# Output bias added to the residual rows by GpSimd instead of by a matmul; two places for the parts of attended rows; one-pass spread of the inverse denominators

## The reference

```python
q = (x @ wq_w.T + wq_b).reshape(b, t, H, HD)      # H = 32 heads of HD = 32
k = (x @ wk_w.T + wk_b); v = (x @ wv_w.T + wv_b)  # one key and value head
scores = jnp.einsum('bqhd,bkd->bhqk', q, k1) / jnp.sqrt(jnp.float32(HD))
scores = jnp.where(causal, scores, -jnp.inf)
attn = jnp.einsum('bhqk,bkd->bqhd', softmax(scores), v1).reshape(b, t, H * HD)
x = _layernorm(x + attn @ wo_w.T + wo_b)          # x: 2 x 2048 x 1024, float32
x_sim = clip(x * x_scale, -448, 448)              # x_scale = 448 / max|x|, w alike
out = _layernorm(x + x_sim @ w_sim * (1 / (x_scale * w_scale)))
```

## Time and profile before

| | |
|---|---|
| runs of the kernel | 2508.66, 2510.32, 2511.88 us; median 2510.32 |
| the profiled execution | 2512.94 us, of which the span of its instructions is 2511.2 |
| PE | busy 2408.2 us, 96% |
| DVE | busy 1750.0 us, 70% |
| ACT | busy 1299.4 us, 52% |
| POOL | busy 802.8 us, 32% |

### The profile page before, as it was taken

One profiled execution on the slowest core, in us unless ns is written; L12 is line 12 of the kernel. 1 busy time (PEld: TensorE's weight loads), 2 busy tenths in 40 slices (PEclk: granted clock), 3 DMA queues, 4 the chain that ended last, 5 costly groups with the idle time before them and its releaser, 6 DMA issues.

```text
span 2511.2 us, 36167 instructions
## 1 busy us (share of the span) xinstructions
PE 2408.2 (96%) x14312; PEld 1559.2 (62%) x14312; DVE 1750.0 (70%) x1294; ACT 1299.4 (52%) x1412; POOL 802.8 (32%) x441
## 2 busy tenths in 40 slices
PE   6999999699999999999999999999999995999998
PEld 5888887245555555555555555555555554888887
DVE  6334335798887888888888888888788884444444
ACT  2222223576777777777776776777777662000000
POOL 2232221022232322232223232322233232556653
PEclk9999999899999999999999999999999997999999
DMA  7433433342232122212222222122212211222221
GB/s 235 142 117 138 154 126 122 94 119 60 74 64 50 43 64 55 54 43 64 51 56 43 52 57 64 43 52 56 65 43 64 51 68 67 84 89 91 88 87 64
DMA packets 150742, 198.01 MB, mean 79 GB/s; under 512 B 8558, under 2 KB 108878, under 8 KB 148558
## 3 DMA queue, kind: packets, MB, share of 16 engines
q1 hardware_dynamic: 126990, 144.71, 22.2%
q10 hardware_dynamic: 23616, 51.39, 5.3%
HBM read 123.72 MB, written 72.35 MB: 78 GB/s over the span
## 4 chain that ended last, share of the span: by engine, by line
PE 66%; DVE 7%; ACT 5%; issue 3%; POOL 1%; ACTq 0%; DVEq 0%; POOLq 0%
PE bank L1233 18%; PE bank L1245 16%; PE bank L1308 14%; PE bank L1218 12%; DVE acc L1000 6%; ACT prob L761 4%; PE bank L1255 2%; PE bank L1263 2%; PE bank L1298 1%; PE bank L1215 1%; ACT att_hi L748 0%; DVE res L974 0%; DVE stats L816 0%; DVE r_den L961 0%; POOL prob L609 0%
## 5 line engine op out<-in xcount | busy, mean ns | idle before, releaser
L761 ACT ACTIVATE prob<-bank 128x1024 f32<-128x1024 f32 x1088 | 1054.9, 1022 | 442.2 <-PE bank L1233 435.3
L1000 DVE TENSOR_TENSOR acc<-acc,prob 128x2048 f32<-128x2048 f32 x420 | 988.3, 2353 | 107.0 <-ACT prob L761 88.7
L1233 PE MATMUL bank<-q_st,keys 98*128 98x512 f32 x2176 | 644.8, 415 | 33.6 <-ACT prob L761 22.1
L1233 PEld LDWEIGHTS bank<-q_st,keys 98*128 98x128 f32 x2176 | 377.0, 189 | 367.9 <-ACT prob L761 264.0
L1245 PE MATMUL bank<-prob,v_t 128*32 128x512 f32 x4352 | 526.3, 602 | 0.0
L609 POOL TENSOR_SCALAR_AFFINE_SELECT prob<-prob 128x1024 f32<-128x1024 f32 x128 | 184.1, 1461 | 736.2 <-ACT prob L761 736.2
L1245 PEld LDWEIGHTS bank<-prob,v_t 128*32 128x32 f32 x4352 | 114.0, 109 | 263.6 <-issue 253.0
L996 DVE TENSOR_TENSOR acc<-prob 128x2048 f32<-128x2048 f32 x60 | 137.6, 2293 | 153.9 <-ACT prob L761 139.5
L1132 PE MATMUL bank<-xt_hi,w_hi 128*128 128x512 f32 x576 | 227.6, 395 | 14.8 <-DVE xt_lo L837 14.1
L1132 PE MATMUL bank<-xt_hi,w_lo 128*128 128x512 f32 x576 | 227.1, 394 | 0.0
L1132 PE MATMUL bank<-xt_lo,w_hi 128*128 128x512 f32 x576 | 226.7, 394 | 0.0
(11 more groups left out here) (112 smaller groups left out, 2555.9 us busy)
## 6 DMA issues: line engine op xcount, KB each, us to landing
q_st<-q_hi_d SPq DMA_DIRECT2D x128, 256.0 KB
xt_raw<-x_t SPq DMA_DIRECT2D x16, 1024.0 KB, 6.9
q_hi_d<-part_hi ACTq DMA_DIRECT2D x64, 256.0 KB, 2.1
q_lo_d<-part_lo ACTq DMA_DIRECT2D x64, 256.0 KB, 2.3
q_st<-q_lo_d SPq DMA_DIRECT2D x64, 256.0 KB
res<-x SPq DMA_DIRECT2D x32, 512.0 KB, 6.0
x_d<-res SPq DMA_DIRECT2D x32, 512.0 KB, 2.7
x<-x_d SPq DMA_DIRECT2D x32, 512.0 KB, 3.3
```

Source lines behind the costliest of these rows:

```text
L761: nc.scalar.activation(prob[:, s % SLOTS, 2 * p:2 * p + 2], bank[:, 2 * p:2 * p + 2], ACT.Exp, scale=SCALE).then_inc(p_done, 1)
L1000: nc.vector.tensor_tensor(acc[:, n % 2], acc[:, n % 2], new, ALU.add).then_inc(acc_done, 1)
L1233: last = nc.tensor.matmul(bank[:, g].rearrange("p (a n) -> p a n", n=P), keys[:, k // QT, k % QT * P:(k % QT + 1) * P], queries[:, :, g], ...
```

## The change

1. **Bias.** The bias matmul of each half is gone, with `share`, `bo_parts` and what made them. `bo` holds the bias in 128 rows, and POOL adds it to each row tile `res` once it is loaded (`add_bias_row`, 32 times), before DVE's `add_residual`, which now waits for that (`res_ready`).
2. **Two places.** `att_hi` and `att_lo` exist twice, by the tile's parity. ACT's split waits for the projection of the tile two before. The odd tile's split stands at step 13 instead of 21; its first half at steps 22 to 28 instead of 24 to 30, its second in five batches, 30 to 38, instead of four, 32 to 38.
3. **Spread.** DVE now rounds the inverse to float32r (`r_hi`) and makes `r_parts`, which holds the rounded inverse in the upper half of each group of rows and its rest in the lower half; `spread` is float32r and picks up both. Its four matmuls are then one-pass.
4. The second place lies where `wf` tiles 2 and 3 go, so those two loads move from step 68 to the tail, behind the projection of `LAST_A`.

```diff
-        spread = sb("spread", [P, QT, P])
+        spread = sb("spread", [P, QT, P], F32R)
+        r_lower = sb("r_lower", [P, 1])
...
-            bo_parts = sb("bo_parts", [P, D], F32R, s)
+            bo = sb("bo", [P, D], F32, s)
...
-                names = (21, 24, 30, 30, 32, 38, 38, 39, 44, 45) if second else (4, 6, 12, 12, 14, 20, 20, 22, 27, 28)
+                names = (13, 22, 28, 28, 30, 38, 38, 39, 44, 45) if second else (4, 6, 12, 12, 14, 20, 20, 22, 27, 28)
...
-                names = (17, 20, 24, 24, 26, 30, 30, 31, END, END) if second else (4, 6, 10, 10, 12, 16, 16, 18, 22, 23)
+                names = (11, 18, 22, 22, 24, 30, 30, 31, END, END) if second else (4, 6, 10, 10, 12, 16, 16, 18, 22, 23)
...
+        row_at = {places(q)[HALF0 if q < LAST_A else SPLIT]: q for q in range(LAST_B)}
...
-            sp.wait_ge(bo_cut, 2)
...
-                if s in split_at:
-                    q = split_at[s]
+                if s in row_at:
+                    q = row_at[s]
...
                     sp.dma_start(res[:, q % 2], x_tiles[tile_row(q)]).then_inc(res_in[q % 2], 16)
...
-                if s == 2 * PAIR:
-                    sp.wait_ge(piece_sent, 16 * KT)
-                    load_wf(2)
-                    load_wf(3)
...
                 sp.dma_start(x1[:, r], x1_d[r]).then_inc(x1_in[r], 16)
+            sp.wait_ge(y_done, 2 * LAST_A + 2)
+            load_wf(2)
+            load_wf(3)
             store_row(LAST_A)
...
+            def add_bias_row(q):
+                pool.wait_ge(res_in[q % 2], 16 * (q // 2 + 1))
+                nc.gpsimd.tensor_tensor(res[:, q % 2], res[:, q % 2], bo[:], ALU.add).then_inc(res_ready, 1)
...
+                if s - 3 in row_at:
+                    add_bias_row(row_at[s - 3])
                 if s in split_at:
                     q = split_at[s]
                     pool.wait_ge(att_hi_cut, q + 1)
-                    nc.gpsimd.tensor_tensor(att_lo[:], att[:, q % TILES_KEPT], att_hi[:].bitcast(F32), ALU.subtract).then_inc(att_cut, 1)
+                    nc.gpsimd.tensor_tensor(att_lo[q % 2][:], att[:, q % TILES_KEPT], att_hi[q % 2][:].bitcast(F32), ALU.subtract).then_inc(att_cut, 1)
...
                 act.wait_ge(att_ready, last_group[q] + 3)
-                act.wait_ge(y_done, 2 * q)
-                nc.scalar.activation(att_hi[:], att[:, q % TILES_KEPT], ACT.Copy).then_inc(att_hi_cut, 1)
+                act.wait_ge(y_done, max(2 * q - 2, 0))
+                nc.scalar.activation(att_hi[q % 2][:], att[:, q % TILES_KEPT], ACT.Copy).then_inc(att_hi_cut, 1)
...
                 dve.wait_ge(den_done, n + 3)
-                nc.vector.reciprocal(r_den[:], bank[:, DEN_BANK, 0:P]).then_inc(den_read, 1)
+                nc.vector.reciprocal(r_den[:], bank[:, DEN_BANK, 0:P]).then_inc(den_inverse, 1)
+                dve.wait_ge(den_inverse, 2 * n + 1)
+                nc.vector.tensor_copy(r_hi[:], r_den[:]).then_inc(den_inverse, 1)
+                dve.wait_ge(den_inverse, 2 * n + 2)
+                nc.vector.scalar_tensor_tensor(out=r_parts[:], in0=r_hi[:].bitcast(F32), scalar=r_lower[:], in1=r_den[:], op0=ALU.mult, op1=ALU.add).then_inc(den_read, 1)
...
-                dve.wait_ge(res_in[q % 2], 16 * (q // 2 + 1))
+                dve.wait_ge(res_ready, q + 1)
...
-                nc.tensor.matmul(dst, share[:], bo_parts[:, cols], start=True, stop=False, skip_group_check=True)
...
-                    last = nc.tensor.matmul(bank[:, DEN_BANK, c * P:(c + 1) * P], spread[:, c], r_den[:], start=True, stop=True)
+                    last = nc.tensor.matmul(bank[:, DEN_BANK, c * P:(c + 1) * P], spread[:, c], r_parts[:], start=True, stop=True)
```

More of the change, by code:

```diff
@@ L548, in _ @@
             nc.gpsimd.memset(head_col[:], 0.0).then_inc(fixed, 1)
[L549 removed]
+            nc.gpsimd.memset(kv[:, TB - 1], 0.0).then_inc(fixed, 1)
             pool.wait_ge(fixed, 2)
@@ L618, in _ @@
                     shift_of(moments[:, q % 2], ln1, q * LN)
+            add_bias_row(LAST_A)
+            add_bias_row(LAST_B)
             for q in (LAST_A, LAST_B):
@@ L1031, in _ @@
             dve.wait_ge(att_hi_cut, LAST_B + 1)
-            nc.vector.tensor_tensor(att_lo[:], att[:, LAST_B % TILES_KEPT], att_hi[:].bitcast(F32), ALU.subtract).then_inc(att_cut, 1)
+            nc.vector.tensor_tensor(att_lo[LAST_B % 2][:], att[:, LAST_B % TILES_KEPT], att_hi[LAST_B % 2][:].bitcast(F32), ALU.subtract).then_inc(att_cut, 1)
             for i in range(1, 4):
@@ L1214, in half_projection @@
                         pe.wait_ge(y_read, 2 * q + half)
-                    nc.tensor.matmul(dst, share[:], bo_parts[:, cols], start=True, stop=False, skip_group_check=True)
                 for at in range(len(todo) * part // parts, len(todo) * (part + 1) // parts):
                     k, a, c = todo[at]
-                    last = nc.tensor.matmul(dst, (att_hi, att_lo)[a][:, k], (wo_hi, wo_lo)[c][:, k, cols],
-                                            start=False, stop=(at == len(todo) - 1), skip_group_check=True)
+                    last = nc.tensor.matmul(dst, (att_hi, att_lo)[a][q % 2][:, k], (wo_hi, wo_lo)[c][:, k, cols],
+                                            start=(at == 0), stop=(at == len(todo) - 1), skip_group_check=True)
                 if part == parts - 1:
```

44 lines of the change are left out of this document (27 added, 17 removed).

## The result

The changed kernel takes 2542.91 us (median of four runs, 2541.39 to 2546.01), the kernel before 2509.49 beside it: a ratio of 1.0134, 95% interval 1.0116 to 1.0151. It is slower by some 33 us, where 2458 us, a gain of 52, was predicted. The profiled execution took 2546.01 us, its span 2544.3. First, from the profile page of the changed kernel, busy time by engine, and the shares of the chain of work that ended last (before, PE had 66% of it and DVE 7%).

The account below looks back on a forecast made before the run. PE was taken as the bound, with an ACT-set floor of about 5.36 us per batch. 2512.9 - 49 (batches) - 5.5 (even tile's wait) - 5.3 (tail) + 5 (DVE contention) = 2458 us; range 2445 to 2484.

Parts of the forecast that it names:

- the term for DVE's contention: POOL's 32 bias additions slow DVE's sums, 1.3 us each by a profile row; put at 5 us, bounds 0 and 43.
- The prediction's own sign: Forecast wrong above all if PE waits over 20 us for add_residual, the spread's operand or masked, or wf splits late.
- additions on the path: Slower rival: each POOL addition holds DVE its whole 2.4 us, and PE with it, 32 times; 2529 us, chance 0.04.
- DVE runs behind: Rival: PE waits 0.5 to 1 us for add_residual at two places per pair, 19 us instead of 5; 2472, chance 0.20.
- as dear as before: First rival: the one-pass spread on PE is no faster than the float32 one; 28 us lost, 2486 us, chance 0.14.
- the second rival: Spread's weight loads on PE hide altogether, so it falls to a quarter, 0.23 us; 2446 us in all, chance 0.08.
- Batch rule: Attention batches take the larger of 5.36 us and PE's own work; summed 1584 us before, 1535 after, gain 49.
- the places: Moving products into each pair's empty batch and spreading the odd tile's second half over five batches gains 10 us.
- Spread: Each one-pass spread in an attention batch costs PE 0.43 us instead of 0.91, worth 28 us.
- it costs nothing unless DVE is late: DVE's two further instructions per group, 0.55 us for 64 groups, fit within 1.27 us of cover before the spread.
- Even tile's wait, 5.5 us: The batch waiting for the even tile's att_lo loses its 0.5 us wait in 11 pairs, with nothing late next.
- Tail, 5.3 us: At the end, LAST_B's late split and slow projection, four bias matmuls and the last spread's cost go: 5.3 us.

Follow-up runs that it names:

- experiment 5: Changed kernel with every instruction and wait kept, but POOL adds only one of the 1024 bias columns: 2485.18 us, ratio 0.9895.
- Experiment 11: Changed kernel with each bias addition on POOL split into four pieces of 256 columns, at successive or later steps: 2514.79 us, ratio 1.001.
- experiment 8: Kernel with two places and one-pass spread, bias matmul kept, with the even tile split at step 3 instead of 4: 2506.59 us, ratio 0.9977.
- 3: Kernel before with only the one-pass spread and its two further DVE instructions: 2505.63 us, ratio 0.998.
- 6: Kernel before with the one-pass spread, the inverse rounded once by the reciprocal, without the two further DVE instructions: 2490.60 us, ratio 0.9913.
- experiment 2: Kernel before with only the two places, the moved odd-tile steps and the late wf loads: 2490.79 us, ratio 0.9918.
- experiment 4: Changed kernel with the bias matmul back and no additions on POOL; two places and one-pass spread stay: 2489.41 us, ratio 0.9913.
- experiment 7: Changed kernel with the 32 bias additions on DVE instead of POOL, at the same steps: 2494.58 us, ratio 0.9928.
- experiment 9: Kernel with two places and one-pass spread, bias matmul kept, with att_lo's subtraction on DVE one step after the split: 2564.73 us, ratio 1.0219.

## Why the prediction was wrong

**The step that failed** is the term for DVE's contention: "I put **5 us** on this". Against experiment 5 the whole additions cost 58 us. The prediction's own sign of it came too: PE waited 49 us for `add_residual` and the spread's operand, where 20 was the limit. Two things were wrong in the term.

First the price of one. I took 1.3 us from a row in which two sums under an `att_lo` took 6.04, and left the rule of the Trainium skill, that the two block each other fully, in a sentence beside it. But that `att_lo` began at 1219.87 and the first sum only at 1220.74, so no more than its last 1.50 us could fall on the sums: the row showed a full hold of a part. Over the whole trace of the changed kernel 25 sums meet an addition and are 2.24 us longer each, 56 us. The Trainium skill, "SBUF — State Buffer", section "Who interferes with whom", states a full block, and this case agrees: 2.24 of an addition's 2.39 us.

Second, what a held microsecond is worth. I set idle DVE time against it: 36 us in four pairs, so nothing would be lost on average. But DVE's results are wanted at fixed places: `add_residual` before a half's first product, the sum before the denominators, the inverse one batch before the spread. DVE runs behind PE there. Experiment 11 has nearly two thirds of the held time (36 us) and half of the loss; experiment 8 moved one 2.4 us hold per pair by a step and lost 16 us; 3 against 6 shows that 0.6 us per group (0.23 and 0.35) cost 15. And a pause of PE can be followed by several microseconds at the lower clock, 58 us in the stage against 3.4, a term that the sum did not have.

**The rivals.** The one with a chance of 0.04, additions on the path at 2529 us, has the mechanism that happened; the time was 2543. It was to decide "from about 1.9 us per addition on", and the row is 2.24. That its number comes near is in part luck: the additions cost 58 us and not its 76, and experiment 5, nearly without them, still stands 27 us above the forecast. Of that the small instructions took some 15, a term that it did not have. "DVE runs behind" had the place right and a third of the price. The one-pass spread came out at half (0.46 for 0.91), neither as dear as before nor at the quarter that the second rival gave it.

**Point by point.**
- *Batch rule.* Right: 48 us by the rule with the measured spread, 49 predicted. In experiment 2 the places gave 10.9, 10 predicted. The prediction's sums of 1584 and 1535 come out again when the batches are counted in the traces; its "57 spreads" does not, since its own table has 56 in batches with products before and 60 after.
- *Spread.* 0.46 against 0.43. But "it costs nothing unless DVE is late" was wrong: DVE was late. Alone it gave 5 us, without the two instructions 19 (experiments 3, 6), and in either the even tile's batch took back a part: it stood 18.4 and 11.8 us above the rule, 6.5 before.
- *Even tile's wait, 5.5 us.* Wrong: ACT's wait is gone, PE's is not, 8.5 us in 11 places; in experiment 2 the batches came 2.7 us nearer to the rule in all, but the even tile's own stood 9.2 us above it instead of 6.5. I had said that ahead of it "stands nothing that could be late next"; `att_lo` on POOL was.
- *Tail, 5.3 us.* About right: experiment 2, which has 3.9 of it (no part 1 or 3), gave 4.9. In the changed kernel 3.2 came (447.1 us from the last batch's start to the end of the span, 450.3 before). PE no longer waits for `LAST_B`'s parts. The last addition stands in the way, in the changed kernel's timeline:

```profile
2112.87 1.06 ACT L766 ACTIVATE att_hi<-att 128x1024 fp32r<-128x1024 f32 x1 [0.33 <-DVE att L995]
...
2115.11 5.69 DVE L1050 TENSOR_TENSOR wf_lo<-wf,wf_hi 128x1024 fp32r<-128x1024 f32 x3
2115.11 3.47 POOL L616 TENSOR_TENSOR res<-res,bo 128x1024 f32<-128x1024 f32 x1 [5.28 <-DMA res<-x]
...
2120.72 0.68 DVE L1002 TENSOR_TENSOR res<-bank,res 128x512 f32<-128x512 f32 x1
```

Three subtractions took 5.69 us, 3.49 in the same place before, and `LAST_A`'s residual stands behind them. That this is where the rest went is not shown: experiment 5, with one column, has a tail of 444.6 us, but experiment 4, without any addition, one of 446.9.

**The sum, redone.** 2511.2 (span before) - 48 (rule) + 88 (107 instead of 19 above the rule) - 3.2 (tail) - 3.4 (up to the second pair, which no term had) = 2544.6, against a span of 2544.3. Of the 88, 64 are waits of PE (76.5 against 12); the other 24 lie in the batches around them. The lower clock is large enough for them: 58 us at half the pace, less 3.4 before, can lose up to 27 us of work. That is an estimate from the clock record, and an upper bound, since a part of these stretches falls on the pauses themselves.

**What stays open.** Pieces of 256 columns halve the loss, but whether by the shorter single hold, by the smaller sum or by the later places is not separated; if the loss went with the held time alone, the 36 us would leave some 37 of the 58 us, and 30 are left. I did not try pieces of other sizes. Why some pauses of PE are followed by the lower clock and others are not is open too (see below). Why experiment 7 came out below my range for theory A I have not looked into further.

## What to carry to other kernels

Before giving an elementwise operation on SBUF to GpSimd, count it at its full length on VectorE's side, and look where VectorE's next result is wanted; if VectorE can do it in less (here 1.36 us against 2.24 held), leave it there, or keep it on TensorE if the bound allows (with parts 2 and 3: 2489 us on TensorE, 2495 on VectorE, 2543 on GpSimd). Idle time alone does not mean room on an engine that is busy for 83% (333 of 400 us): ask at each place where another engine waits for it how much earlier than needed its result is there. A rule on batch lengths gives the gain of a change to the bound, but not what its helpers take back; measure the parts apart.

## What was not expected of the hardware

- The blocking goes both ways and is nearly complete: `att_lo` needs 2.36 us and lasted 3.98 beside a sum in experiment 8; a sum needs 2.29 and lasted 4.24 beside an `att_lo` in the changed kernel.
- Small pieces on POOL take turns with DVE: 256 columns lasted 0.73 us at the least and 2.78 in the median (48 of them), nearly all of it waiting for a sum to end.
- After a pause of 4.80 us TensorE's granted clock was 0.50 for 3 us and 0.72 for the next 4; after one of 4.85 us in experiment 9 products again followed at 0.43 us. Short pauses can do it too: nine of the 13 stretches at the lower level in the changed kernel follow pauses of 1.6 to 2.8 us. Eight others of 1.5 to 1.7 us were followed by none, so the length alone does not decide.
- A one-pass spread of four matmuls of 128 columns costs 0.46 us in a batch, 0.115 each, so a quarter of the columns costs half of the 0.23 that a product of 512 takes.
